# Layer 0's product taken from a transposed x three tiles ahead, with the channel mix applied to the product; phase-major x and output

## The chip, the cores and the metric

One core of a Trainium2 chip runs the program. The metric is the time of one execution in microseconds on the device; medians of several executions are compared. The profile is that of one execution, whose span runs from the first to the last instruction.

## The reference

Two layers are applied to x (128 batches, 32 channels, 512 features). Each mixes channels or features of a batch and then applies a linear layer over the 512 features with a low-rank part that is chosen per row; both add their result to x.

```python
# layer 0: per-batch channel mix, then linear + 4 gated low-rank experts
agg_w = einsum('bk,koi->boi', att, weight)          # 32x32 per batch, att from an MLP on cond_128
c0 = einsum('boi,bih->boh', agg_w, x) + agg_b[:, :, None]
y0 = c0 @ W_base.T + b_base + sum_e alpha_e * ((c0 @ A_e.T) @ B_e.T) * 2
x1 = x + y0                                         # alpha = softmax over 4 experts of c0 @ router_W
# layer 1: grouped convolution of 9 taps along the features, then linear + top 2 of 28 experts
c1 = conv(x1, weight, groups=4) + ctx + bias
y1 = c1 @ base_W.T + sum_{top 2} gate_e * ((c1 @ A_e.T) @ B_e.T) * 2
out = x1 + y1
```

## The kernel before

A tile is 4 batches, so its 128 rows are 4 x 32 channels; there are 32 tiles (NT). Every engine runs its own program and waits on semaphores. Each has a function `step(s)`, and `steps` calls it for s = -1 or 0 to 33: the first and last ones unrolled, the middle in a loop of four steps. In step s TensorE works on layer 0 of tile s, the convolution of tile s-1, and layer 1 of tiles s-2 (LAG) and s-3. So the order of the calls in `step` is the order of TensorE's work; nothing else plans it.

Layer 0 of tile t goes so. `mix` holds for each tile a block-diagonal 128x128 matrix with the four batches' agg_w. Four plain fp32 matmuls (L866) with a quarter of x as the stationary operand give c0 transposed in `p_c0`. ScalarE rounds it to f32r (`c0_hi`, L478), VectorE takes the rest (`c0_lo`, L620). The linear layer is then done in three f32r passes, hi x hi, hi x lo (`hi_passes`, L713 and L714) and lo x hi (`lo_passes`, L719), over 4 chunks of 128 features: first half with 36 columns for experts and router (292 columns, into `p_y0a`), then `other_half` (256 columns). The router chain on VectorE and ScalarE (L601 to L616, L473) makes g0s; TensorE transposes it (L897), ScalarE copies it to g0t (L487), and two matmuls (L916, L917) add the low-rank part and the biases. VectorE adds x (L638, two halves) to give x1.

x1 goes to a scratch in memory (L365) and comes back as convolution windows (L355, three DMAs). The convolution is 16 plain fp32 matmuls with 32-column stationary operands (L790). VectorE transposes its result (L595), ScalarE rounds it (L470), GpSimd takes the rest (L432). `lows_1` multiplies by 224 low-rank and 28 gate columns (252 columns), VectorE does the top-2 gate chain (L671 to L696), `base_1` is the linear layer (512 columns, 12 matmuls), `transpose_g1` (L804) and `low_rank_1` (6 matmuls of 512 columns) finish the tile, and VectorE adds x1 into `y_sb` (L585), which is stored (L362). x and the output are stored feature by feature, while the kernel works by phase (feature mod 4): L585 and L638 read or write with a stride of 4.

Before step 0 comes a setup: a small MLP on TensorE and ScalarE gives att; eight f32r matmuls (L757) on a stack of hi and lo parts of the weights give all mix matrices, which VectorE (L563) and ScalarE (L461) copy into `mix` in 16 blocks each; eight matmuls (L725, L726) pick the active experts; row sums and biases are folded into b0_stack and z_add (L646, L652); w0, a1 and w1 are split into hi and lo parts on ScalarE, GpSimd and VectorE (L454, L412, L490, L492, L655, L428); b1_hi and b1_lo are made from three matmuls (L923, L927, L928).

## Time and profile before

| what | us |
|---|---|
| median of 3 runs (402.69 to 403.41) | 403.36 |
| span of the profiled execution | 401.6 |
| TensorE busy (share) | 384.2 (96%) |
| VectorE busy | 269.5 (67%) |
| ScalarE busy | 97.4 (24%) |
| GpSimd busy | 77.4 (19%) |
| share of the chain that ended last: TensorE | 90% |
| DMA: 54.65 MB, share of the 16 engines' time | 57.1% |

The profiled execution's own time on the device is not listed apart from its span; the span lies 1.8 us under the median, since it counts from the first instruction to the last and the time of a run also has what lies around them. In the rows further down, a line of the timeline is a start, a duration, the engine, the line of the kernel, the operation, its output and inputs, and a count; in brackets stands the idle time before it and what ended it. A plain fp32 matmul leaves two records, an f32r one a single record. Matmuls overlap, so their pace is read from one start to the next and not from a duration.

### The profile page before, as it was taken

How to read it: one execution, taken by the hardware profiler on the slowest of the kernel's cores; microseconds unless marked ns; L12 is line 12 of the kernel's file. 1: busy time of each engine (PE TensorE's matmuls, PEld its weight loads, DVE VectorE, ACT ScalarE, POOL GpSimd, SP SyncE). 2: the span in 40 equal slices, each digit the busy share in tenths (PEclk: the TensorE clock that was granted, in tenths of full speed). 3: DMA queues.
4: the chain of work that ended last, by engine and by line, in shares of the span. 5: the costliest groups of instructions: out<-in, count | busy, mean ns of one | idle time of the engine just before them, and what ended most of it. 6: DMA issues, size and time to landing. Idle time of an engine off the chain costs nothing.

```text
span 401.6 us, 9219 instructions
## 1 busy us (share of the span) xinstructions
PE 384.2 (96%) x3233; PEld 334.9 (83%) x3233; DVE 269.5 (67%) x891; ACT 97.4 (24%) x287; POOL 77.4 (19%) x124
## 2 busy tenths in 40 slices
PE   4799899999999999999999999999999999999986
PEld 3667788888889988888889988888889888888774
DVE  6696376767766666667766666667766666667655
ACT  5742222211122222211122222211122222212120
POOL 5764111110111111110111111110111111110120
PEclk9999999999999999999999999999999999999999
DMA  7604766565566566655566666655566666654441
GB/s 257 220 2 95 169 132 154 136 146 133 124 153 139 123 157 157 145 127 133 123 153 137 124 157 157 144 125 135 125 153 135 126 157 157 145 125 114 101 95 52
DMA packets 65699, 54.65 MB, mean 136 GB/s; under 512 B 3357, under 2 KB 52733, under 8 KB 65430
## 3 DMA queue, kind: packets, MB, share of 16 engines
q1 hardware_dynamic: 65686, 54.48, 57.1%
q8 instruction: 7, 0.11, 0.1%
q14 instruction: 6, 0.05, 0.1%
HBM read 37.56 MB, written 16.91 MB: 136 GB/s over the span
## 4 chain that ended last, share of the span: by engine, by line
PE 90%; DVE 4%; DMA 2%; issue 2%; ACT 1%; SPq 0%; POOL 0%; DVEq 0%
PE p_y L713 10%; PE p_y L714 10%; PE p_y L719 10%; PE p_y0ab L713 9%; PE p_y0ab L719 8%; PE p_y0ab L714 8%; PE p_cv L790 8%; PE p_c L866 7%; PE p_h L719 4%; PE p_h L713 4%; PE p_h L714 4%; PE p_g L804 2%; DMA win<-x_scratch 1%; PE p_y0ab L916 1%; PE p_c L897 1%
## 5 line engine op out<-in xcount | busy, mean ns | idle before, releaser
L432 POOL TENSOR_TENSOR c_lo<-c,c_hi 128x512 fp32r<-128x512 f32 x32 | 40.7, 1273 | 253.3 <-ACT c_hi L470 253.3
L713 PE MATMUL p_y0ab<-w_hi,c_hi 128*128 128x292 f32 (+1 forms) x256 | 73.9, 316 | 0.5 <-DVE x L638 0.5
L714 PE MATMUL p_y0ab<-w_lo,c_hi 128*128 128x292 f32 (+1 forms) x256 | 67.6, 290 | 0.0
L713 PEld LDWEIGHTS p_y0ab<-w_hi,c_hi 128*128 128x128 f32 x256 | 48.7, 190 | 9.5 <-issue 8.0
L585 DVE TENSOR_TENSOR y_sb<-p_y,x 128x512 f32<-128x512 f32 x31 | 33.5, 1080 | 32.7 <-PE p_y L719 32.7
L713 PE MATMUL p_y<-w_hi,c_hi 128*128 128x512 f32 x124 | 49.4, 398 | 0.0
L714 PEld LDWEIGHTS p_y0ab<-w_lo,c_hi 128*128 128x128 f32 x256 | 49.1, 192 | 0.0
L714 PE MATMUL p_y<-w_lo,c_hi 128*128 128x512 f32 x124 | 49.0, 395 | 0.0
L719 PE MATMUL p_y0ab<-w_hi,c_lo 128*128 128x292 f32 (+1 forms) x256 | 43.1, 290 | 0.0
L470 ACT CAST c_hi<-c 128x512 fp32r<-128x512 f32 x32 | 19.8, 620 | 89.9 <-DVE c L595 89.9
L498 ACT ACTIVATE t_exp<-top,ntop 128x2 f32<-128x2 f32 x32 | 9.5, 296 | 129.6 <-DVE ntop L678 129.6
L638 DVE TENSOR_TENSOR x<-p_y0ab,x_sb 128x256 f32<-128x256 f32 x64 | 35.6, 598 | 3.5 <-PE p_y0ab L917 3.5
L790 PEld LDWEIGHTS p_cv<-win,wc_sb 96*32 96x32 f32 x1024 | 26.0, 109 | 13.7 <-issue 10.7
L719 PEld LDWEIGHTS p_y0ab<-w_hi,c_lo 128*128 128x128 f32 x256 | 36.7, 190 | 0.0
L790 PE MATMUL p_cv<-win,wc_sb 96*32 96x128 f32 x1024 | 34.6, 276 | 1.8 <-DMA win<-x_scratch 1.8
L866 PE MATMUL p_c<-mix,x_sb 128*128 (+1 forms) x256 | 35.4, 283 | 0.0
L719 PE MATMUL p_y<-w_hi,c_lo 128*128 128x512 f32 x124 | 34.0, 396 | 0.0
L866 PEld LDWEIGHTS p_c<-mix,x_sb 128*128 128x128 f32 x256 | 33.3, 199 | 0.0
L713 PE MATMUL p_h<-a_hi,c_hi 128*128 128x252 f32 x128 | 31.7, 281 | 0.0
L714 PE MATMUL p_h<-a_lo,c_hi 128*128 128x252 f32 x128 | 31.5, 280 | 0.0
L595 DVE STREAM_TRANSPOSE c<-p_cv 128x512 f32<-128x512 f32 x32 | 22.9, 716 | 12.1 <-PE p_cv L790 12.1
L601 DVE TENSOR_TENSOR z<-p_y0ab,z_add 128x36 f32<-128x36 f32 x32 | 6.2, 194 | 34.9 <-PE p_y0ab L719 34.9
(182 smaller groups left out, 683.2 us busy)
## 6 DMA issues: line engine op xcount, KB each, us to landing
win<-x_scratch SPq DMA_DIRECT2D x96, 256.0 KB, 4.4
x_scratch<-x SPq DMA_DIRECT2D x32, 260.0 KB, 2.1
x_sb<-in_x SPq DMA_DIRECT2D x32, 256.0 KB, 5.1
out<-y_sb SPq DMA_DIRECT2D x32, 256.0 KB, 2.1
w_sb<-in_w SPq DMA_DIRECT2D x2, 1024.0 KB, 8.6
exp_sb<-in_experts SPq DMA_DIRECT2D x1, 512.0 KB, 4.7
a_sb<-in_a SPq DMA_DIRECT2D x1, 504.0 KB, 8.1
b_sb<-in_b SPq DMA_DIRECT2D x1, 448.0 KB, 11.7
```

What stands on the lines that cost most here:

```text
L432: pool.tensor_tensor(by_group(c1_lo[:, v.mod(2)]), by_phases(c1), by_group(c1_hi[:, v.mod(2)].bitcast(f32)), ALU.subtract).then_inc(c1_lo_ ...
L470: nc.scalar.copy(by_group(c1_hi[:, v.mod(2)]), by_phases(c1)).then_inc(c1_hi_done, 1)
L498: nc.scalar.activation(t_exp[:], top[:, 0:2], ACT.Exp, bias=ntop[:], accum_out=t_sum[:]).then_inc(t_exp_done, 1)
L585: V.tensor_tensor(y_sb[:, v.mod(2), :].rearrange("p (q f) -> p f q", f=NPH), y1_bank(v).rearrange("p (f q) -> p f q", f=NPH), x1[:, v.mod( ...
L595: V.transpose(c1[:], p_cv[:]).then_inc(c1_tr, 1)
L638: last = V.tensor_tensor(x1[:, s.mod(4), phases, 1:1 + NQ], p_y0[n].rearrange("p (f q) -> p f q", q=NQ), x_sb[:, s.mod(4), :].rearrange("p ...
L713: mm(psum, lhs_hi, rhs_hi, start=start and n == 0, stop=False)
L714: mm(psum, lhs_hi, rhs_lo, start=False, stop=False)
L719: last = mm(psum, lhs_lo, rhs_hi, start=False, stop=stop and n == len(operands) - 1)
L790: last = mm(p_cv[rows, :].rearrange("p (b g m) -> p b g m", b=BT, g=GROUPS)[:, :, g], wc_sb[:, g, :], win[:, v.mod(2)].rearrange("p (b g) ...
L804: last = nc.tensor.transpose(p_g1t[:, a, :], g1[:, a, :], ident[:])
L866: last = mm(p_c0[:, cols], x_sb[:, t.mod(4), cols], mix[:, t.n(), :], start=True, stop=True)
```

## The change

Layer 0's linear layer and channel mix are exchanged: mixing acts on the rows and the linear layer on the features, so (mix x) W = mix (x W). The host passes x also transposed (`xt`), 128 features by 128 rows for each of 4 chunks. TensorE computes u = x W in three f32r passes with the quarters of xt as stationary operands (`u_half`, halves "b" and "a") three tiles ahead (UA), ScalarE rounds xt (`xt_high`) and copies u out of PSUM (`u_copy`), GpSimd takes xt's low part (`xt_low`) and copies the tile's mix matrix (`mix_copy`). In step s two plain fp32 matmuls of 292 and 256 columns (`mixing`) apply the mix matrix to u. Step 0 computes u of tiles 1, 2 and 3, and u of tile 0 is computed in the setup; steps 29 to 31 compute none.

In the setup, seven matmuls of `ones` by `ones`, whose result nobody reads, come first on TensorE. w0 is loaded in four quarters that ScalarE and VectorE split; the f32r stack of the attention weights is gone, and eight plain fp32 matmuls take its place. The mix blocks are copied in two parts, those of tiles 0 to 3 in the setup and the others in step 0; z_add likewise. w1 is loaded into w0's buffer once that is free, and split in step 1; b1 comes with a row of zeros from the host, which a row sum of w1 fills in step 2, instead of three matmuls. x and the output are phase-major in memory (the host rearranges them), so that both additions on VectorE are one contiguous operation of 512 columns; the addition of x now comes after the gate chain on VectorE. `at(s, c)` is true in the unrolled step c. Layer 1's computation is the same, but its gate product comes before u and its transpose at the step's end.

```diff
+            sp.dma_start(xt_sb[:, 0, :], xt[0]).then_inc(xt_loaded[0], 16)
+            for c in range(HC):
+                sp.dma_start(w_sb[:, c, :], w0[:, c * D:(c + 1) * D]).then_inc(ld_w0[c], 16)
...
+            sp.dma_start(xt_sb[:, 1, :], xt[1]).then_inc(xt_loaded[1], 16)
+            sp.dma_start(bb_sb[:], b_base).then_inc(ld_bb, 16)
+            sp.dma_start(xt_sb[:, 2, :], xt[2]).then_inc(xt_loaded[2], 16)
             sp.dma_start(x_sb[:, 0, :], x_v[0]).then_inc(x_loaded[0], 16)
+            sp.dma_start(xt_sb[:, 3, :], xt[3]).then_inc(xt_loaded[3], 16)
...
+            sp.wait_ge(xt_lo_done, 1)
+            sp.dma_start(xt_sb[:, 0, :], xt[4]).then_inc(xt_loaded[0], 16)
+            sp.wait_ge(w0_lo_done, HC)
+            sp.wait_ge(w0_pairs_done, 1)
+            sp.dma_start(w_sb[:], w1.rearrange("p (c d) -> p c d", c=HC)).then_inc(ld_w1, 16)
+            sp.wait_ge(a0_mm, 1)
+            sp.wait_ge(b0_mm, 1)
+            sp.dma_start(b1_sb, b1.rearrange("p (a d) -> p a d", a=2)).then_inc(ld_b1, 16)
...
+                if (s + 5).live():
+                    t = s + 5
+                    after(sp, xt_lo_done, t, -4)
+                    sp.dma_start(xt_sb[:, t.mod(4), :], xt[t.n()]).then_inc(xt_loaded[t.mod(4)], 16)
...
+            def xt_low(t):
+                after(pool, xt_hi_done, t)
+                pool.tensor_tensor(xt_lo[:, t.mod(2)], xt_sb[:, t.mod(4)], xt_hi[:, t.mod(2)].bitcast(f32),
+                                   ALU.subtract).then_inc(xt_lo_done, 1)
...
+                after(pool, mixed_mm, t, -4)
+                pool.tensor_copy(mix_t[:, t.mod(4)], mix[:, t.n(), :]).then_inc(mixt_done, 1)
...
+                if at(s, 0):
+                    xt_low(s + 3)
+                if (s + 2).live():
+                    mix_copy(s + 2)
+                if (s + 4).live():
+                    xt_low(s + 4)
...
+            def xt_high(t):
+                after_dma(act, xt_loaded, t)
+                after(act, u_mm, t, -2, 2, 2)
+                nc.scalar.copy(xt_hi[:, t.mod(2)], xt_sb[:, t.mod(4)]).then_inc(xt_hi_done, 1)
+            def u_copy(t, half):
+                part, (banks, cols) = "ba".index(half) + 1, HALVES[half]
+                after(act, u_mm, t, 0, 2, part)
+                after(act, mixed_mm, t, -4)
+                nc.scalar.copy(u[:, t.mod(4), cols], p_u[:, banks]).then_inc(u_done, 1)
...
+                t = s + (1 if at(s, 0) else UA)
+                if t.live():
+                    u_copy(t, "b")
+                if s.live():
+                    after(act, g0_tr, s)
+                    nc.scalar.copy(g0t[:], p_g0t).then_inc(g0t_done, 1)
+                if t.live():
+                    u_copy(t, "a")
+                if at(s, 0):
+                    act.wait_ge(mix_zeroed, 5)
+                    for n, t in enumerate((s + 2, s + 3)):
+                        u_copy(t, "b")
+                        u_copy(t, "a")
+                        if n == 0:
+                            xt_high(s + 4)
+                        mix_copies(REST, [n])
...
                     after_dma(dve, y_stored, v, -2)
-                    V.tensor_tensor(y_sb[:, v.mod(2), :].rearrange("p (q f) -> p f q", f=NPH),
+                    V.tensor_tensor(y_sb[:, v.mod(2), :].rearrange("p (f q) -> p f q", f=NPH),
                                     y1_bank(v).rearrange("p (f q) -> p f q", f=NPH), x1[:, v.mod(4), :, 1:1 + NQ],
                                     ALU.add).then_inc(y_done, 1)
+                def residual(v):
+                    after(dve, y0_mm, v)
+                    after_dma(dve, x_loaded, v)
+                    after_dma(dve, x1_stored, v, -4)
+                    V.tensor_tensor(x1[:, v.mod(4), :, 1:1 + NQ], p_x1.rearrange("p (f q) -> p f q", q=NQ),
+                                    x_sb[:, v.mod(4), :].rearrange("p (f q) -> p f q", f=NPH), ALU.add).then_inc(x1_done, 1)
...
+                if s.live():
+                    residual(s)
+                if at(s, 0):
+                    dve.wait_ge(mix_zeroed, 5)
+                    mix_copies(REST, range(BT // 2, BT))
...
+                    dve.wait_ge(rs1_mm, 1)
+                    V.tensor_copy(rs1[:], p_rs1).then_inc(rs1_done, 1)
+                    dve.wait_ge(a1_hi_done, 1)
+                    V.tensor_tensor(a1_lo[:], a1_sb[:], a1_hi[:].bitcast(f32), ALU.subtract).then_inc(a1_lo_done, 1)
+                    dve.wait_ge(w1_hi_done, 1)
+                    V.tensor_tensor(w1_lo[:], w_sb[:], w1_hi[:].bitcast(f32), ALU.subtract).then_inc(w1_lo_done, 1)
...
+            def u_operands(t, cols):
+                slot = t.mod(2)
+                return [(xt_hi[:, slot, c * P:(c + 1) * P], xt_lo[:, slot, c * P:(c + 1) * P], w0_hi[:, c, cols], w0_lo[:, c, cols])
+                        for c in range(HC)]
+            def u_half(t, half):
+                part, (banks, cols) = "ba".index(half) + 1, HALVES[half]
+                after(pe, xt_hi_done, t)
+                after(pe, u_done, t, -1, 2, part)
+                hi_passes(p_u[:, banks], u_operands(t, cols), True)
+                after(pe, xt_lo_done, t)
+                lo_passes(p_u[:, banks], u_operands(t, cols), True).then_inc(u_mm, 1)
...
+            pe.wait_ge(ones_done, 1)
+            for _ in range(7):
+                mm(p_u[:, 0:P], ones[:], ones[:], start=True, stop=True)
...
+            after(pe, xt_hi_done, first)
+            for c in range(HC - 1):
+                pe.wait_ge(w0_lo_done, c + 1)
+                hi_passes(p_u[:, banks], u_operands(first, cols)[c:c + 1], c == 0)
+            pe.wait_ge(ident_done, 1)
+            pe.wait_ge(att_done, 1)
+            nc.tensor.transpose(p_att, att[:], ident[:]).then_inc(att_t_mm, 1)
+            pe.wait_ge(w0_lo_done, HC)
+            hi_passes(p_u[:, banks], u_operands(first, cols)[HC - 1:HC], False)
+            after(pe, xt_lo_done, first)
+            lo_passes(p_u[:, banks], u_operands(first, cols), True).then_inc(u_mm, 1)
...
             pe.wait_ge(att_t_done, 1)
             for m in range(CH // BT):
-                last = mm(p_y0ab[:, m * BATCH:(m + 1) * BATCH], kw_stack[:, m * BT * CH:(m + 1) * BT * CH], att_t[:],
+                last = mm(p_cvh[:, m * BATCH:(m + 1) * BATCH], kw_sb[:, m * BT * CH:(m + 1) * BT * CH], att_t[:],
                           start=True, stop=True)
...
+            pe.wait_ge(a0_lo_done, 1)
+            u_half(first, "a")
             pe.wait_ge(vmat_done, 1)
-            mm(p_vrow, vmat[:], sel_r[:], start=True, stop=True).then_inc(vrow_mm, 1)
+            mm(p_vrow, vmat[:], sel_r[:], start=True, stop=True)
+            pe.wait_ge(a0_sum_done, 1)
+            mm(p_rs0, ones[:], a0_sum[:], start=True, stop=True).then_inc(zrow_mm, 1)
+            pe.wait_ge(beta1_done, 1)
+            mm(p_b0, sel[:], exp_sb[:, 1, :], start=True, stop=False)
+            pe.wait_ge(w0_sum_done, 1)
+            pe.wait_ge(picks_done, 2)
+            mm(p_b0, pick_rs0[:], w0_sum[:], start=False, stop=False)
...
+                def mixing(v):
+                    if at(v, 0):
+                        pe.wait_ge(rs0_done, 1)
+                        pe.wait_ge(vrow_done, 1)
+                    after(pe, u_done, v, 0, 2, 2)
+                    after(pe, mixt_done, v)
+                    after(pe, x1_done, v, -1)
+                    for half in "ab":
+                        banks, cols = HALVES[half]
+                        mm(p_y0[:, banks], mix_t[:, v.mod(4)], u[:, v.mod(4), cols], start=True,
+                           stop=half == "a").then_inc(z0_mm if half == "a" else mixed_mm, 1)
...
                 if s.live():
-                    after(pe, c0_lo_done, s)
...
-                if s.live():
-                    after(pe, x1_done, s, -1)
-                    first = [(*c0_pairs[c], w0_hi[:, c, 0:Z0N + NY], w0_lo[:, c, 0:Z0N + NY]) for c in range(HC)]
-                    hi_passes(p_y0a[:, 0:Z0N + NY], first, True)
-                    lo_passes(p_y0a[:, 0:Z0N + NY], first, True).then_inc(z0_mm, 1)
-                if (s + 1).live():
-                    t = s + 1
-                    after_dma(pe, x_loaded, t)
-                    if t.i is None and t.c in (0, 1):
-                        pe.wait_ge(mix_act_done, (t.c + 1) * BT * BT // 2)
-                        pe.wait_ge(mix_dve_done, (t.c + 1) * BT * BT // 2)
-                    after(pe, c0_lo_done, s)
-                    for c in range(HC):
-                        cols = slice(c * P, (c + 1) * P)
-                        last = mm(p_c0[:, cols], x_sb[:, t.mod(4), cols], mix[:, t.n(), :], start=True, stop=True)
-                    last.then_inc(c0_mm, 1)
...
+                    mixing(s)
+                if at(s, 0):
                     pe.wait_ge(ld_bb, 16)
-                    mm(p_y1[0:K0, :], pick_rs0[:], w0_sum[:], start=False, stop=False)
-                    mm(p_y1[0:K0, :], pick_bias[:], bb_sb[:], start=False, stop=True).then_inc(b0_mm, 1)
...
-                if (s + -LAG).live() and is_last(s + -LAG):
+                    mm(p_b0, pick_bias[:], bb_sb[:], start=False, stop=True).then_inc(b0_mm, 1)
...
-                if (s + -LAG).live() and not is_last(s + -LAG) and not lows_early:
-                    lows_1(s + -LAG)
-                conv_early = s.i is None and s.c >= NT - 1
-                if (s + -1).live() and conv_early:
-                    conv(s + -1)
-                if (s + -LAG).live() and not is_last(s + -LAG):
-                    base_1(s + -LAG)
-                if (s + -1).live() and not conv_early:
-                    conv(s + -1)
-            steps(pe, step, -1, NT + 2, 3, 7)
+                    low_rank_1(s + -LAG)
+                else:
+                    if (s + -3).live() and not is_last(s + -3):
+                        low_rank_1(s + -3)
+                    if (s + -LAG).live():
+                        lows_1(s + -LAG)
+                    ahead = (s + 1, s + 2, s + 3) if at(s, 0) else (s + UA,)
+                    running = ahead[0].live()
+                    if running:
+                        for n, t in enumerate(ahead):
+                            u_half(t, "b")
+                            if n == 0:
+                                transpose_g0(s)
+                            u_half(t, "a")
+                            if n == 0:
+                                low_rank_0(s)
+                    elif s.live():
+                        transpose_g0(s)
+                    if at(s, 1):
+                        pe.wait_ge(a1_sum_done, 1)
+                        mm(p_rs1, ones[:], a1_sum[:], start=True, stop=True).then_inc(rs1_mm, 1)
+                    if (s + -LAG).live():
+                        if not running and s.live():
+                            base_1(s + -LAG, lambda: low_rank_0(s))
+                        elif is_last(s + -1):
+                            base_1(s + -LAG, lambda: conv(s + -1))
+                        else:
+                            base_1(s + -LAG)
+                    if (s + -1).live() and not is_last(s + -1):
+                        conv(s + -1)
+                    if (s + -LAG).live():
+                        transpose_g1(s + -LAG)
+                if at(s, 2):
+                    pe.wait_ge(b1_lo_done, 1)
+            steps(pe, step, 0, NT + 1, 3, 6)
...
+    rows = i["x"].reshape(NT, P, HC, P)
     return {
-        "x": c(i["x"]), "pack": pack, "kw": c(kw), "experts": c(experts.reshape(P, -1)),
+        "x": by_phase(i["x"]), "xt": c(rows.transpose(0, 3, 2, 1)).reshape(NT, P, HC * P), "pack": pack, "kw": c(kw),
...
+    phased = r.results[0]["out"].reshape(BATCH, CH, NPH, NQ)
+    return np.ascontiguousarray(phased.swapaxes(-1, -2)).reshape(BATCH, CH, D)
```

Three places show the new order. The first is TensorE in the steady loop, where one step ends and the next begins; before the change, around the channel mix:

```order
L719 MATMUL p_y0ab<-w_hi,c_lo 128x292 x4
L866 ISA
L866 MATMUL p_c<-mix,x_sb 128x128 x4
L804 MATMUL p_g<-ident,g 113x128 x2
L713 MATMUL p_y0ab<-w_hi,c_hi 128x256
```

After the change, from the convolution to the low-rank part of layer 1:

```order
L943 MATMUL p_cvh<-win,wc_sb 32x4x32 x16
L956 MATMUL p_t<-ident,g 113x128 x2
L309 REGISTER_ALU
L913 MATMUL p_y<-u,mix_t 128x292
L913 MATMUL p_y<-u,mix_t 128x256
L808 MATMUL p_y<-b_hi,g1t_hi 128x512
```

The mix has moved from between the two halves of the product to the head of the step, behind the transposes of layer 1's gates, and has become two wider matmuls.

The second place is TensorE in the setup, from the picking of experts on. Before:

```order
L757 MATMUL p_y0ab<-att_t,kw_stack 128x128 x8
L761 MATMUL p_cv<-att_t,kw_stack 32x32 x4
...
L768 MATMUL p_g<-sel_r,vmat 128x4
L866 MATMUL p_c<-mix,x_sb 128x128 x4
L873 MATMUL p_c<-a_sum,ones 128x36
L875 MATMUL p_y<-exp_sb,sel 101x512
L713 MATMUL p_y0ab<-w_hi,c_hi 128x292
```

After:

```order
L881 MATMUL p_cvh<-att_t,kw_sb 128x128 x8
L885 MATMUL p_t<-att_t,kw_sb 32x32 x4
L808 MATMUL p_u<-w_hi,xt_hi 128x292
...
L814 MATMUL p_u<-w_hi,xt_lo 128x292 x4
L892 MATMUL p_y<-sel_r,vmat 128x4
L894 MATMUL p_y<-a_sum,ones 128x36
L896 MATMUL p_y<-exp_sb,sel 101x512
L899 MATMUL p_y<-w_sum,pick_rs 101x512
L913 MATMUL p_y<-u,mix_t 128x292
```

Tile 0's product now stands in the setup, half "b" ahead of the picking of experts and half "a" behind the attention matmuls, and the mixing of tile 0 closes the setup.

The third place is VectorE between the router chains of tiles 0 and 1. Before:

```order
L626 SCALAR_TENSOR_TENSOR b_stack<-b_round,minus_lo_row,p_y 101x512
L638 TENSOR_TENSOR x<-p_y0ab,x_sb 128x2x128 x2
L658 COPY rs<-p_g 128x252
L661 TENSOR_TENSOR b_lo<-p_cv,b_hi 113x512
L601 TENSOR_TENSOR z<-p_y0ab,z_add 128x36
```

After:

```order
L736 SCALAR_TENSOR_TENSOR b_stack<-b_round,minus_lo_row,p_y 101x512
L698 TENSOR_TENSOR x<-p_y,x_sb 128x4x128
L624 COPY mix<-p_cvh 32x28x8 x8
L629 TENSOR_TENSOR z_add<-rs,beta 128x1008
L632 TENSOR_TENSOR z_add<-z_add,vrow 128x28x4
L716 TENSOR_TENSOR z<-p_y,z_add 128x36
```

The mix blocks of tiles 4 to 31 and 28 rows of z_add have moved from the setup to a place between two tiles.

## Rows read from the trace of the kernel before

**Rows 1.** The page, parts 1 and 2: busy time of each engine, TensorE by slice, granted clock.

```profile
PE 384.2 (96%) x3233; PEld 334.9 (83%) x3233; DVE 269.5 (67%) x891; ACT 97.4 (24%) x287; POOL 77.4 (19%) x124
...
PE   4799899999999999999999999999999999999986
...
PEclk9999999999999999999999999999999999999999
```

**Rows 2.** Timeline of TensorE, one tile from 200 us: start, duration, engine, line, operation.

```profile
200.29 0.41 PE L713 MATMUL p_y0ab<-w_hi,c_hi 128*128 128x292 f32 x1
...
202.01 1.06 PE L866 MATMUL p_c<-mix,x_sb 128*128 x8
202.90 0.38 PE L804 MATMUL p_g<-ident,g 128*113 128x128 f32 x2
...
204.57 0.48 PE L713 MATMUL p_y<-b_hi,g1t_hi 113*128 113x512 f32 x1
...
207.69 0.40 PE L713 MATMUL p_y<-w_hi,c_hi 128*128 128x512 f32 x1
...
210.58 1.08 PE L790 MATMUL p_cv<-win,wc_sb 96*32 96x128 f32 x32
211.59 0.41 PE L713 MATMUL p_y0ab<-w_hi,c_hi 128*128 128x292 f32 x1
```

**Rows 3.** Timeline of TensorE in setup and the first tiles.

```profile
11.80 1.93 PE L757 MATMUL p_y0ab<-att_t,kw_stack 24*128 24x128 f32 x8 [0.46 <-DVE att_t L552]
...
13.92 0.64 PE L725 MATMUL p_h<-sel,exp_sb 128*128 128x32 f32 x2
...
16.50 2.08 PE L866 MATMUL p_c<-mix,x_sb 128*128 128x128 f32 x8
...
21.41 2.01 PE L875 MATMUL p_y<-exp_sb,sel 128*101 128x512 f32 x2
23.34 0.61 PE L713 MATMUL p_y0ab<-w_hi,c_hi 128*128 128x292 f32 x1
...
26.43 1.62 PE L866 MATMUL p_c<-mix,x_sb 128*128 128x128 f32 x8
...
38.92 1.02 PE L927 MATMUL p_h<-b_sb,ident 112*113 112x512 f32 x2
39.78 1.02 PE L928 MATMUL p_h<-w_sum,pick_rs 128*113 128x512 f32 x2
```

**Rows 4.** Timeline of VectorE, the same tile from 200 us.

```profile
202.33 0.20 DVE L601 TENSOR_TENSOR z<-p_y0ab,z_add 128x36 f32<-128x36 f32 x1 [1.18 <-PE p_y0ab L719]
...
204.09 0.19 DVE L616 TENSOR_TENSOR g0s<-g,g0s 128x32 f32<-128x32 f32 x1
...
208.19 0.24 DVE L671 SCALAR_TENSOR_TENSOR h<-rs,beta,p_h 128x28 f32<-128x28 f32 x1
...
210.95 0.39 DVE L696 TENSOR_TENSOR g<-h,gate 128x224 f32<-128x224 f32 x1
```

**Rows 5.** Groups of instructions by line and shape: line, operation, count, busy us, mean ns, idle before.

```profile
L620 DVE TENSOR_TENSOR c_lo<-p_c,c_hi 128x512 fp32r<-128x512 f32 x32 | 21.8, 683 | 0.0
...
L655 DVE TENSOR_TENSOR a_lo<-a_sb,a_hi 128x1008 fp32r<-128x1008 f32 x1 | 1.2, 1194 | 0.0
...
L575 DVE TENSOR_TENSOR beta<-beta 128x32 f32<-128x32 f32 x1 | 0.8, 784 | 0.0
...
L461 ACT COPY mix<-p_y0ab 32x224 f32<-32x224 f32 x8 | 4.4, 545 | 0.2
...
L492 ACT CAST w_hi<-w_sb 128x2048 fp32r<-128x2048 f32 x1 | 1.9, 1912 | 0.0
...
L432 POOL TENSOR_TENSOR c_lo<-c,c_hi 128x512 fp32r<-128x512 f32 x32 | 40.7, 1273 | 253.3 <-ACT c_hi L470 253.3
```

**Rows 6.** Timelines of VectorE and TensorE near the end.

```profile
376.41 1.13 DVE L638 TENSOR_TENSOR x<-p_y0ab,x_sb 128x256 f32<-128x256 f32 x2
...
385.79 1.08 PE L790 MATMUL p_cv<-win,wc_sb 96*32 96x128 f32 x32 [0.53 <-DMA win<-x_scratch]
```

496 lines of the change are left out of this document (229 added, 267 removed).

## The prediction

> **What bounds the kernel now.** I read the page first. TensorE is busy for 384.2 of the 401.6 us of the span, VectorE for 269.5 [rows 1], so the next question is what TensorE does in one tile and what it loses at the two ends. In the timeline of TensorE in the middle of the run the same instruction comes back after 11.30 us (200.29 to 211.59) [rows 2], and the slices of TensorE read 9 (90% or more) from the sixth to the third last [rows 1]. Inside the period the starts follow one another without a gap: first half of the layer-0 product with its logit columns 1.72 us (200.29 to 202.01), channel mix 0.89 us (202.01 to 202.90), second half with three transposes 1.67 us, low-rank parts of both layers and the low-rank-and-gate product of layer 1 together 3.12 us (by their columns 1.45, 0.24 and 1.43), its base product 2.89 us (207.69 to 210.58), convolution 1.01 us [rows 2]. TensorE is the bound of the tile, and no wait is left there that a new order could remove. What lies outside 32 periods (32 x 11.30 = 361.6) is 40 us: setup, filling and draining the pipeline.
>
> At the start TensorE runs at its lower level (1.2 GHz). The page's row of granted clock shows full speed from the first slice [rows 1], but the intervals contradict it: eight records of the channel mix take 2.08 us at 16.50 and 1.06 us in the steady part, and the twelve matmuls of the first half 3.09 us (23.34 to 26.43) against 1.72. The mix at 26.43 takes 1.62 us, so the level (2.4 GHz from then on) rose inside it, near 27.3 [rows 2, 3]. The useful stream of tile 0 begins at 23.34.
>
> **The steady tile after the change.** Removed: the channel mix on x, 0.89 us. Added: two plain fp32 matmuls of 292 and 256 columns on the product. A plain fp32 matmul of 512 columns takes 0.86 us (38.92 to 39.78) [rows 3], that is 1.68 ns a column, so 548 columns cost 0.92 us. Everything else TensorE does per tile stays. New period: 11.30 - 0.89 + 0.92 = 11.33 us. For the period I take bounds of 11.21 (the convolution is now followed by transposes, and the late start of the f32r matmul after it, 0.12 us of the 1.72, may go) and 11.45 (that much added instead).
>
> Could the new order wait? I walk one step, S = start of the mixing matmuls. They end at S+0.92, layer 1's low rank at S+2.4, its gate product at S+3.8, half b of the product three tiles ahead at S+5.3, half a at S+6.9, layer 0's low rank at S+7.2, base at S+10.1, convolution at S+11.1. VectorE begins, as now, with the transpose of the convolution and g1t_lo, to about S+1.15; then comes the layer-0 router chain of 1.95 us (202.33 to 204.28) [rows 4] to S+3.1; its transpose is asked for at S+5.3. Output addition: the contiguous layout makes it like c_lo, 0.68 us [rows 5], to S+3.8. Gate chain of 3.15 us (208.19 to 211.34) [rows 4] from S+4.05 to S+7.2; its transpose is asked for at S+11.1. Residual 0.68 us to S+8.0; the next mixing wants it at S+11.3. ScalarE gains two copies of the product and one rounding of x and loses one rounding: some 4.1 us of work a step. GpSimd gains x's low part, like the 1.27 us of c_lo [rows 5], and a copy of a quarter of that size. Both stay far under 11.3 us. All slacks are over 0.6 us, the shortest being g0t on ScalarE (ready S+6.3, wanted S+6.9). So the drop in VectorE's work (0.68 of c_lo and 0.4 twice) buys nothing here. The extra load of 256 KB a tile and the rest of the DMAs wait for semaphores that were posted a step before, on SP's queue as well; I cost them at nothing.
>
> **The setup, up to the first mixing (T0).** In the kernel before, the attention chain reaches its matmuls at 11.80 [rows 3]. In the new one the first projection stands behind seven warm-up matmuls (14 records of 0.25 us, ending near 4.7), and VectorE and ScalarE weave four quarters of w0's rounding into the chain; I put the last quarter's low part at 12.5. From there TensorE has: 6 matmuls to finish half b of tile 0; the 8 expert and router matmuls (0.53 us each at the lower level, by the rows at 13.9) [rows 3]; 8 plain fp32 matmuls of 128 columns, i.e. 16 records (0.25 us each at the lower level, 0.111 at the higher) instead of 8; bias rows; half a; two small ones; two of 512 columns. At the higher level: 12.5 + 0.7 + 2.1 + 1.8 + 0.2 + 1.6 + 0.4 + 1.7 = 21.0. At the lower level all of it would be 12.5 + 1.4 + 4.2 + 4.0 + 0.4 + 2.9 + 0.9 + 3.7 = 30.0. Which one holds depends on whether the warm-up matmuls and what follows them raise the level. I take 21.0: the warm-ups run straight into the first projection, so the engine works without a pause from 1.1 to about 5.4, 4.3 us, and the level rose about 4 us after the first matmul of the dense stream at 23.34 [rows 3]; after that no long pause follows. Against it: there, TensorE had been working since 21.0 without the level rising for over 6 us, and what ran first was plain fp32, as the warm-ups are.
>
> The trace cannot decide this. The Trainium skill, "TensorE: Matmul & The Clock Gate" (Part 1), says the default state is throttled and sustained activity releases the throttle. By that rule T0 is 21.0; the rows of the kernel before show only that the level rose late in its own setup.
>
> **The first three steps.** Step 0 holds mixing 0.92, bias row 0.86, three products of 3.1 and low rank 0.24: 11.4 us. Meanwhile VectorE and ScalarE copy the remaining mix blocks, eight each at 0.55 us [rows 5], and VectorE builds 28 rows of z_add, so tile 1's router chain starts near T0+14.9 and its transpose comes at T0+16.5: TensorE waits 2.6 us. Step 1 ends at T0+20.0. Then lows_1 of tile 0 needs the transposed convolution, and on VectorE that is queued behind a1_lo (1.19) and w1_lo (twice as long), which wait for a1_hi and w1_hi (1.91) on ScalarE [rows 5]: it comes at T0+25.6, a wait of 3.7 us. Step 3 begins at T0+35.0. The b1 matmuls of the kernel before (about 2.6 us) are gone; one row sum of 0.86 takes their place.
>
> **The end.** Steps 3 to 28 take 26 x 11.33 = 294.6. Steps 29 and 30 have no product left: 8.24 each, plus a window wait of 0.9: 17.4. x1 of tile 31 comes 7.95 later. From x1 done (377.54) to the last convolution (385.79) it takes 8.25 us, two DMA trips [rows 6]; that path is unchanged and now has less work beside it. After that convolution 15.8 us remained; eight of the twelve matmuls of a base product (1.87) now lie before it and the output addition is 0.4 shorter, but 0.8 more is waited for c1_lo: 14.3.
>
> Sum: 21.0 + 35.0 + 294.6 + 17.4 + 7.95 + 8.25 + 14.3 = 398.5 us of span, against 401.6: 3.1 us less. The median of the three runs, 403.36, lies 1.8 above the profiled span; with the same 1.8 the forecast is **400.3 us**. So three tiles of product moved into the pipeline's start save time at the start, and about half is given back in waits of the first steps and at the end.
>
> **Rivals.** A difference of 0.2% (0.8 us) is about what a measurement tells from none.
> (1) *The clock stays low during setup* (slower). The 14 warm-up records are plain fp32 and the matmuls after them are small and spread; if the level rises only near 24, in half a, T0 is 12.5 + 1.4 + 4.2 + 4.0 + 0.4 + 2.2 + 0.5 + 1.7 = 26.9, and with some waiting 27.3: 406.6 us. It decides from T0 = 24.1 on. For it: the level was low through 7 us of small matmuls (11.8 to 18.6) in the kernel before.
> (2) *VectorE is slowed by GpSimd in the steady tile* (slower). Row L575 took 0.78 us for 32 elements while GpSimd was adding, where L616 took 0.19 for the same size [rows 4, 5]. GpSimd works 3 us per tile in place of 1.7, over the router chain. If its five short operations took 0.6 more each, the chain would end at S+6.1, and TensorE would wait 0.8 us: 26 times, 421.3 us. Against it: the chain has 2.2 us of slack first, and operations that read PSUM were not stretched. By the Trainium skill, "GPSIMD Engine Reference" (1. Specifications), GpSimd shares its SBUF interfaces with VectorE and contends with operations with two SBUF inputs; that agrees with L575.
> (3) *The tile gets cheaper* (faster): 11.21 us each, 26 x 0.12 = 3.1 less: 397.2 us.
>
> **Chances and range.** Forecast 50%, own range 397 to 403 (2.5 for the walk through setup, 1 for the period); rival 1 34%, 404 to 409; rival 2 6%; rival 3 10%. Of the forecast's half 0.43 is faster, 0.04 same, 0.03 slower; rival 3 adds 0.10 to faster; rival 1 0.02 to same and 0.32 to slower; rival 2 0.06. That is 0.53, 0.06, 0.41. The range from 395.5 to 407.5 leaves out rival 2, the upper end of rival 1 and little below.
>
> **What would show it.** Right: warm-ups' successors at 0.11 us per record by 15 us; mixing of tile 0 near 21; starts of the mixing matmuls 11.33 apart; a wait for VectorE's z chain of tile 1 and a longer one before lows_1 of tile 0; the last convolution waiting for its window. Wrong: mixing of tile 0 after 24.1, a period off 11.33 by over 0.1, or waits for x1 in the loop.

## The result

| kernel | median us (lowest to highest, runs) | span of the profiled execution |
|---|---|---|
| before | 403.13 (402.69 to 403.41, 4) | 401.6 |
| changed | 428.80 (428.69 to 429.74, 4) | 427.1 |

The changed kernel takes 1.0646 times as long (95% interval 1.0631 to 1.0661): 25.7 us slower, where 400.3 was forecast. The sum of the prediction, 398.5 us of span, is 28.6 us short. It was made in four pieces, and each can be read from the starts of the mixing matmuls (L913), which stand at 32.25 for tile 0, 80.24 for tile 3, 378.77 for tile 29 and 396.17 for tile 31:

| piece | forecast | measured | difference |
|---|---|---|---|
| setup, to the first mixing (T0) | 21.0 | 32.25 | +11.25 |
| steps 0 to 2 | 35.0 | 47.99 | +13.0 |
| steps 3 to 28 (26 periods) | 26 x 11.33 = 294.6 | 26 x 11.48 = 298.5 | +3.9 |
| steps 29 and 30, and the end | 17.4 + 30.5 | 17.4 + 30.9 | +0.4 |

```profile
32.25 1.29 PE L913 MATMUL p_y<-u,mix_t 128*128 128x292 f32 x4
...
80.24 1.09 PE L913 MATMUL p_y<-u,mix_t 128*128 128x292 f32 x4
...
378.77 1.09 PE L913 MATMUL p_y<-u,mix_t 128*128 128x292 f32 x4
...
396.17 1.09 PE L913 MATMUL p_y<-u,mix_t 128*128 128x292 f32 x4
```

The profile's page of the changed kernel, against [rows 1], shows more busy time on TensorE and a clock that dips in two places:

```profile
PE 397.5 (93%) x3123; PEld 336.0 (79%) x3123; DVE 275.1 (64%) x829; ACT 117.2 (27%) x352; POOL 118.0 (28%) x187
...
PE   5698619999999999999999999999999999999976
...
PEclk9559967999999999999999999999999999999999
```

Cut at the places where the granted clock changes or a step begins, the stretches that matter read so (stretch, length, busy us and instructions of TensorE, its weight loads, VectorE, ScalarE and GpSimd, mean granted clock, share of the DMA engines, GB/s):

```profile
5.30:8.70 3.40, 1.27 (x6) 0.89 (x6) 1.77 (x6) 1.88 (x5) 1.26 (x1) 1.00 0.95 303
8.70:15.00 6.30, 2.05 (x6) 1.08 (x5) 5.67 (x8) 2.41 (x5) 5.76 (x4) 0.50 0.99 370
15.00:32.20 17.20, 17.13 (x66) 14.07 (x67) 7.01 (x21) 3.12 (x12) 4.76 (x8) 0.50 0.20 64
...
45.50:56.50 11.00, 4.55 (x31) 3.93 (x29) 3.80 (x9) 3.85 (x10) 2.71 (x4) 1.00 0.06 25
56.50:70.10 13.60, 7.40 (x42) 3.57 (x42) 9.05 (x11) 5.40 (x10) 10.21 (x8) 0.50 0.76 162
```

Three things stand in it. From 15.0 to 32.2 TensorE works without a pause, at 1.2 GHz: the level had risen at 5.3 us and was gone at 8.7. From 45.5 to 56.5 every engine idles most of the time while the DMA engines are at a share of 0.06, that is one sixteenth. And from 56.5 to 70.1 the clock is low again. The waits of TensorE name what it idled for (us in total, times, longest):

```profile
PE p_cvh L943 <- DMA win<-x_scratch: 7.4, 4, 5.3
PE p_y L929 <- ACT g0t L559: 6.3, 2, 5.1
PE p_u L808 <- DVE w_lo L617: 5.5, 4, 2.3
```

**Step 1 (45.56 to 66.20).** The wait of 5.1 us for g0t is put down to ScalarE, but ScalarE was waiting too, for a load. Its timeline:

```profile
56.20 0.62 ACT L489 CAST xt_hi<-xt_sb 128x512 fp32r<-128x512 f32 x1 [7.01 <-DMA xt_sb<-in_xt]
56.84 0.37 ACT L496 COPY u<-p_u 128x256 f32<-128x256 f32 x1
57.11 0.27 ACT L559 CAST g0t<-p_t 101x128 fp32r<-101x128 f32 x1
```

The queue of SP, which issues the loads and stores, shows what stood ahead of that load:

```profile
34.64 0.25 SPq L364 DMA_DIRECT2D exp_sb<-in_b  x1
34.94 5.67 SPq L376 DMA_DIRECT2D x_sb<-in_x  x1
40.66 1.20 SPq L380 DMA_DIRECT2D xt_sb<-in_xt  x1
41.90 1.26 SPq L387 DMA_DIRECT2D x_scratch<-x  x1
56.90 1.51 SPq L373 DMA_DIRECT2D win<-x_scratch  x3
```

b1 is issued at 34.64, into 113 partitions (112 rows and the new row of zeros). What follows it on the same queue needs 5.67 us to be issued, the transposed x of tile 5 (xt, issued by 41.9) arrives near 56.2, 14 us after its issue, and the store of x1 of tile 0, issued by 43.2, is only done at 56.9, when the windows can be read. For most of the time in between, from 46.5 to 54.5, the DMA engines move 26 GB/s:

```profile
46.50:54.50 8.00, 3.55 (x26) 3.10 (x24) 2.80 (x9) 2.57 (x6) 1.79 (x3) 1.00 0.06 26
```

At that rate (25 GB/s) the 452 KB of b1 take 18 us, from about 36 to 54. My theory (A) was that this one load is carried by one engine. The rival (B): the queue was backed up by bytes.

**The steady tile.** Four mixings in a row are 11.45, 11.45, 11.45 and 11.60 us apart. In one tile of the changed kernel the pieces from one start to the next are: g1's transposes 0.31, mixing 0.74, layer 1's low-rank part (`low_rank_1`) 1.57, its 252 low-rank and gate columns (`lows_1`) 1.39, half b with g0's transpose 1.46, half a 1.73, layer 0's low rank 0.34, base 2.89, convolution 1.01. Taken over the region from g1's transposes to the end of half b, without g0's transpose (0.03), that is 5.44 us, against 4.52 for the same pieces before: the mixing costs 0.92 as forecast. Most of the surplus is at layer 0's low rank, 0.34 in place of 0.24. TensorE there, ScalarE and VectorE, from three timelines:

```profile
211.82 0.27 PE L922 MATMUL p_t<-ident,g0s 128*101 128x128 f32 x1
...
213.58 0.38 PE L929 MATMUL p_y<-b_stack,g0t 101*128 101x256 f32 x1
213.80 0.28 PE L930 MATMUL p_y<-b_stack,g0t 101*128 101x256 f32 x1
```

```profile
212.72 0.30 ACT L552 ACTIVATE t_exp<-top,ntop 128x2 f32<-128x2 f32 x1 [3.77 <-DVE ntop L756]
...
213.01 0.35 ACT L496 COPY u<-p_u 128x256 f32<-128x256 f32 x1
213.26 0.27 ACT L559 CAST g0t<-p_t 101x128 fp32r<-101x128 f32 x1
```

```profile
209.70 1.23 DVE L728 CAST g0s<-g 128x64 fp32r<-128x64 f32 x1
```

g0 is transposed at 211.82, but its copy waits on ScalarE behind the exponential of layer 1's top two (`t_exp`), which waits for VectorE. g0t is ready at 213.53, and the weight load that needs it cannot run ahead. VectorE is late because its cast of the gates takes 1.23 us (0.20 before, as a group 1.035 against 0.195) while GpSimd makes c's and x's low parts.

### The profile page after: what moved, and what is told of

The parts are those of the page before. It is cut to its first block, busy times and chain, and to the rows that moved or that the text cites. A ratio compares the mean times of both kernels' runs of the same rounds, so it can differ in the third digit from the quotient of the medians.

```text
span 427.1 us, 9296 instructions
## 1 busy us (share of the span) xinstructions
PE 397.5 (93%) x3123; PEld 336.0 (79%) x3123; DVE 275.1 (64%) x829; ACT 117.2 (27%) x352; POOL 118.0 (28%) x187
## 4 chain that ended last, share of the span: by engine, by line
PE 79%; DMA 8%; DVE 5%; issue 3%; SPq 2%; ACT 1%; POOL 0%; POOLq 0%; DVEq 0%; ACTq 0%
PE p_y L808 9%; PE p_y L814 9%; PE p_y L809 9%; PE p_cvh L943 7%; PE p_u L814 7%; PE p_u L808 7%; PE p_u L809 7%; PE p_y L913 6%; DMA x_scratch<-x 4%; PE p_cvh L814 3%; PE p_cvh L808 3%; DMA win<-x_scratch 3%; PE p_cvh L809 3%; PE p_t L956 3%; PE p_y L929 2%
## 5 line engine op out<-in xcount | busy, mean ns | idle before, releaser
L808 PE MATMUL p_u<-w_hi,xt_hi 128*128 128x256 f32 (+1 forms) x256 | 71.9, 306 | 5.5 <-DVE w_lo L617 5.5
L809 PE MATMUL p_u<-w_lo,xt_hi 128*128 128x256 f32 (+1 forms) x256 | 68.4, 293 | 0.0
L808 PEld LDWEIGHTS p_u<-w_hi,xt_hi 128*128 128x128 f32 x256 | 49.1, 192 | 7.3 <-DVE w_lo L617 4.7
L809 PEld LDWEIGHTS p_u<-w_lo,xt_hi 128*128 128x128 f32 x256 | 49.2, 192 | 0.0
L420 POOL TENSOR_TENSOR xt_lo<-xt_sb,xt_hi 128x512 fp32r<-128x512 f32 x32 | 41.2, 1288 | 24.5 <-ACT xt_hi L489 24.5
L814 PE MATMUL p_u<-w_hi,xt_lo 128*128 128x256 f32 (+1 forms) x256 | 43.8, 294 | 0.0
L943 PE MATMUL p_cvh<-win,wc_sb 96*32 96x128 f32 x1024 | 35.4, 280 | 7.4 <-DMA win<-x_scratch 7.4
L814 PEld LDWEIGHTS p_u<-w_hi,xt_lo 128*128 128x128 f32 x256 | 37.4, 193 | 0.0
L913 PE MATMUL p_y<-u,mix_t 128*128 128x256 f32 (+1 forms) x128 | 36.2, 406 | 0.0
L728 DVE CAST g0s<-g 128x64 fp32r<-128x64 f32 x32 | 33.1, 1035 | 1.1
L808 PE MATMUL p_cvh<-a_hi,c_hi 128*128 128x252 f32 x128 | 31.4, 280 | 1.0 <-ACT c_hi L539 1.0
L698 DVE TENSOR_TENSOR x<-p_y,x_sb 128x512 f32<-128x512 f32 x32 | 21.9, 685 | 12.2 <-PE p_y L930 12.0
```

Source lines behind the costliest of these rows:

```text
L420: pool.tensor_tensor(xt_lo[:, t.mod(2)], xt_sb[:, t.mod(4)], xt_hi[:, t.mod(2)].bitcast(f32), ALU.subtract).then_inc(xt_lo_done, 1)
L698: V.tensor_tensor(x1[:, v.mod(4), :, 1:1 + NQ], p_x1.rearrange("p (f q) -> p f q", q=NQ), x_sb[:, v.mod(4), :].rearrange("p (f q) -> p f q ...
L728: V.tensor_copy(g0s[:, 0:3 * L0N].rearrange("p (a n) -> p a n", n=L0N)[:, 0:3:2, :].bitcast(f32r), g0[:].unsqueeze(1).to_broadcast([P, 2, ...
L808: mm(psum, lhs_hi, rhs_hi, start=start and n == 0, stop=False)
L809: mm(psum, lhs_hi, rhs_lo, start=False, stop=False)
L814: last = mm(psum, lhs_lo, rhs_hi, start=False, stop=stop and n == len(operands) - 1)
```

## The experiments

The four causes were taken apart first, each with one edit of the changed kernel (428.80 us, T0 32.25, mixing of tile 3 at 80.24, period 11.48).

**e1_b1_rows.** b1 in two loads:

```diff
-sp.dma_start(b1_sb, b1.rearrange("p (a d) -> p a d", a=2)).then_inc(ld_b1, 16)
+sp.dma_start(b1_sb[1:K1], b1[1:K1].rearrange("p (a d) -> p a d", a=2)).then_inc(ld_b1, 16)
+sp.dma_start(b1_sb[0:1], b1[0:1].rearrange("p (a d) -> p a d", a=2)).then_inc(ld_b1, 16)
```

> The load of b1 (113 rows of 4 KB) is split into one of 112 rows and one of a single row; nothing else differs from the changed kernel (428.8 us). Theory A: the load into 113 rows is carried by one of the 16 DMA engines (from about 36 to 54 us the trace shows 25 GB/s at a DMA share of 0.06, one sixteenth), and the loads and the store queued behind it on that engine land only after it. Split, x of tile 5 lands before 46 us, TensorE's waits of 5.07 us (g0t) and 5.27 us (first window) go, about 11 us; the wait before the first low-rank product of layer 1 that was forecast (3.7 us) then appears: 418 to 421 us. Rival B: the queue is backed up by the bytes ahead of it (1 MB of w1 and b1 itself), whatever their rows: 427.5 to 430 us, both waits as before.

Measured: 424.60 us (423.81 to 429.72), ratio to before 1.0577 (1.0509 to 1.0645). SP's queue, and what the 8 us from 46.5 look like now:

```profile
34.88 0.33 SPq L364 DMA_DIRECT2D exp_sb<-in_b  x1
...
35.59 0.35 SPq L377 DMA_DIRECT2D x_sb<-in_x  x1
...
42.72 1.41 SPq L374 DMA_DIRECT2D win<-x_scratch  x3
```

```profile
46.50:54.50 8.00, 2.64 (x18) 2.40 (x17) 6.07 (x9) 3.93 (x10) 6.41 (x6) 0.92 0.36 89
```

The same 452 KB no longer hold anything up: the next issue takes 0.35 us in place of 5.67, and the windows are asked for at 42.72 in place of 56.90. Theory A stands, B falls. Both waits that it named are gone, and the step from the second to the third mixing takes 12.76 in place of 20.64. But the time fell by 4.2 us and not by 8 to 11, for two new waits came: 3.08 us before layer 1's first low-rank product, as forecast, and one that was not, 5.36 us for g0s of tile 1 on VectorE (2.31 in the changed kernel). VectorE and GpSimd in that wait:

```profile
51.34 2.26 DVE L732 TENSOR_TENSOR g0s<-g,g0s 128x32 f32<-128x32 f32 x1
```

```profile
51.22 2.34 POOL L434 TENSOR_TENSOR w_pair<-w_sb 128x1024 f32<-128x1024 f32 x1
```

An operation that takes 0.19 us by itself ends at 53.60, that of GpSimd at 53.56; the cast before it (1.18 us) ends in the same way with GpSimd's low part of x. With the load out of the way GpSimd gets to w1's sum just when VectorE works on the gates. Of the 42.6 us that the three steps still take, step 0 has 13.1, step 1 12.8 and step 2 16.7, where the forecast had 11.4, 8.6 and 15.0: what is left of the miss stands mainly in step 1.

**e2_fill.** Matmuls on `ones` in TensorE's pauses of the setup, 7 behind the attention scores, 10 behind the second quarter of tile 0's half b, 5 behind the transpose of the attention weights:

```diff
+def filler(n):
+    for _ in range(n):
+        mm(p_cvh[:, 0:P], ones[:], ones[:], start=True, stop=True)
...
+filler(7)
...
+filler(10)
...
+filler(5)
```

> 22 more 128x128 plain fp32 matmuls on ones, into columns of a PSUM tile that is not yet used: 7 after the attention scores, 10 after the second quarter of tile 0's product, 5 after the transpose of the attention weights. They fill TensorE's pauses of 1.6, 2.3 and 1.3 us between 6.7 and 15.1 us. Theory A: the granted clock fell to 1.2 GHz at 8.7 us because TensorE paused; with the pauses filled it stays at 2.4 GHz, the 17.2 us from 15.0 to the first mixing take some 8.5, and the first mixing starts near 23.7: 419 to 422 us. Rival B: the narrow matmuls of the setup (4 to 128 columns) bring the level down, or keep it down, whatever came before: first mixing at 30 to 33, 427 to 430 us.

Measured: 423.77 us (422.64 to 425.55), ratio 1.0528 (1.0501 to 1.0556). The first mixing is at 26.48, between the two theories. Two of the stretches of 5 us; the granted clock is the number before the DMA share:

```profile
5.00:10.00 5.00, 4.01 (x22) 3.82 (x23) 2.98 (x10) 3.45 (x8) 1.68 (x2) 0.74 0.95 315
...
20.00:25.00 5.00, 5.00 (x32) 4.43 (x31) 2.00 (x10) 2.57 (x10) 0.29 (x1) 0.66 0.01 5
```

The level still fell before 10 us (the pauses of the attention chain, 0.79 and 0.46 us, had no fillers) and again at 21.1. That second fall came with no pause of TensorE since 15.45, behind a dense half of a product and then matmuls of 4, 32 and 128 columns. So filling the pauses gave 5.8 us of T0 and did not hold the level; that the narrow matmuls brought it down is what their place suggests, no run without them shows it.

**e3_g0t_first.** On ScalarE the exponential behind g0t:

```diff
-if (s + -LAG).live():
-    after(act, ntop_done, s, -LAG)
-    nc.scalar.activation(t_exp[:], ...)
...
 if s.live():
     after(act, g0_tr, s)
     nc.scalar.copy(g0t[:], p_g0t).then_inc(g0t_done, 1)
+if (s + -LAG).live():
+    after(act, ntop_done, s, -LAG)
+    nc.scalar.activation(t_exp[:], ...)
```

> On ScalarE the exponential of layer 1's top two (which waits for VectorE's gate chain) is put behind the copy of the transposed gates of layer 0 (g0t), which TensorE waits for. Theory A: the steady tile takes 11.48 us in place of 11.33 because g0t is copied at 213.26, behind the exponential that came free at 212.72, while its transpose was done near 211.95: period 11.33 to 11.36, about 3.5 to 4 us less in all: 424.5 to 425.5 us. Rival B: the extra 0.15 us is the price of going from plain fp32 to f32r and back: within 0.5 us of 428.8, period 11.45 to 11.48.

Measured: 427.31 us (425.00 to 429.60), ratio 1.0621 (1.0568 to 1.0673). By the times alone this is not told from the changed kernel. The median is in neither expected range, and the runs spread over 4.6 us. The trace does tell: from the fourth mixing to tile 29 every period is 11.32 or 11.33 us, and g0t is copied 0.47 us after its transposition started, not 1.44:

```profile
210.35 0.27 PE L922 MATMUL p_t<-ident,g0s 128*101 128x128 f32 x1
...
212.08 0.29 PE L929 MATMUL p_y<-b_stack,g0t 101*128 101x256 f32 x1
```

```profile
210.82 0.27 ACT L555 CAST g0t<-p_t 101x128 fp32r<-101x128 f32 x1
```

Theory A stands: the price of the exchange in the steady tile is the forecast 0.03 us, the other 0.15 was a queue. The span of this execution, 423.2, is 3.9 us less than 427.1, about what 26 x 0.15 gives.

**e4_sum_late.** GpSimd's sums of w0 moved:

```diff
 xt_low(Tile(None, 0))
-for c in range(HC):
-    pool.wait_ge(ld_w0[c], 16)
-sum_chunks(w_sb, w_pair[:], w0_pairs_done, w0_sum, w0_sum_done)
 xt_low(Tile(None, 1))
+pool.wait_ge(w0_lo_done, HC)
+sum_chunks(w_sb, w_pair[:], w0_pairs_done, w0_sum, w0_sum_done)
```

> GpSimd's sum of the four quarters of w0 (2.41 and 1.60 us, from 9.2 us on) is moved behind the last low part of w0 on VectorE. Theory A: VectorE's low part of the third quarter took 2.72 us in place of 0.69 because GpSimd was adding; moved, it takes 0.69, the last quarter is ready near 12.5 in place of 15.0, and the first mixing comes 2 to 2.7 us earlier: 425.8 to 427 us. Rival B: the sums and the load of w1 behind them come late for their users, or another wait of setup takes its place: within 0.7 us of 428.8.

Measured: 424.01 us (422.64 to 427.20), ratio 1.0508 (1.0479 to 1.0538). VectorE's low part of the third quarter, in the changed kernel and here:

```profile
9.40 2.72 DVE L617 TENSOR_TENSOR w_lo<-w_sb,w_hi 128x512 fp32r<-128x512 f32 x1
```

```profile
9.63 0.69 DVE L616 TENSOR_TENSOR w_lo<-w_sb,w_hi 128x512 fp32r<-128x512 f32 x1
...
11.63 0.67 DVE L616 TENSOR_TENSOR w_lo<-w_sb,w_hi 128x512 fp32r<-128x512 f32 x1
```

The last quarter is done at 12.30 in place of 15.02, and the first mixing starts at 29.53 in place of 32.25: 2.72 us in both places, theory A to the digit. The profiled execution came out at 425.4 us of span, 1.7 less than the changed kernel, and the median 4.8 less, more than the 1.8 to 3 expected; with the runs spread over 4.6 us the size of the gain at the end stays less certain than that at T0.

**e5_xt_late.** The other way to the steady tile:

```diff
 if (s + 4).live():
+    after(pool, g0_lo_done, s)
     xt_low(s + 4)
```

> The changed kernel with one wait more on GpSimd: the low part of x (1.29 us a tile) begins only after VectorE's layer-0 router chain of the same step, ScalarE's order as it was. Theory A: the period of 11.45 to 11.48 us comes from GpSimd: its subtraction beside the chain stretches VectorE's small operations (the cast of the gates takes 1.23 us in place of 0.19), the logits of layer 1, the exponential behind them and with it g0t come late. Without the overlap the cast takes under 0.7 us and the period is 11.33 to 11.36: 424.5 to 426 us. Rival B: g0t is late by the order on ScalarE alone, and the chain's stretch is covered by other waits: period still 11.45 or more, within 0.7 us of 428.8.

Measured: 425.15 us (421.59 to 429.87), ratio 1.0508 (1.0456 to 1.0560). Periods 11.32 to 11.34 throughout. VectorE's cast:

```profile
208.32 0.20 DVE L729 CAST g0s<-g 128x64 fp32r<-128x64 f32 x1
```

So the two explanations of the steady tile are links of one chain: GpSimd's extra operation lengthens the cast by 1.03 us, VectorE's gate chain starts that much later, the exponential and with it g0t too. Breaking it at either link gives 11.33.

**e6_no_warm.** `for _ in range(7)` before the first projection becomes `range(0)`.

> The changed kernel without its seven warm-up matmuls. Theory A: they buy 2.4 GHz from 5.3 to 8.7 us only, in which TensorE does little but wait for w0's quarters, so nothing is lost without them: 427.5 to 429.5 us, first mixing at 32 to 32.5. Rival B: what they set off matters later, and without them the level stays low beyond 32.6 us: 430 to 434 us.

Measured: 428.61 us (427.13 to 434.26), ratio 1.0605 (1.0584 to 1.0626). Theory A: seven warm-ups with nothing dense behind them bought nothing that these runs can tell. In the profiled execution the first mixing came later, at 34.11, by a mishap on VectorE that shows the coupling with GpSimd at its plainest: 8 elements a partition took 4.18 us, until 17.49, beside a subtraction of GpSimd's and its four memsets, the last of which ended at 17.46. The granted clock rose only at 31.9 us here; the level of 5.3 to 8.7 us was the warm-ups'.

```profile
13.31 4.18 DVE L651 TENSOR_SCALAR att<-am_exp,am_rec 128x8 f32<-128x8 f32 x1
```

```profile
14.27 3.19 POOL L443 MEMSET mix<- 128x896 f32 x4
```

**e7_four.** The edits of e1, e3 and e4 together, and fillers of 3, 2, 7 and 4 matmuls, now also in the pauses of the attention chain.

> Four edits together: b1 loaded as 112 rows and one, w0's sums on GpSimd behind VectorE's low parts, g0t ahead of layer 1's exponential on ScalarE, and fillers on TensorE (3, 2, 7 and 4 matmuls of 128 columns in the pauses up to 12 us). If the four causes are independent, their gains add: first mixing at 21 to 24 us, mixing of tile 3 some 42.6 later (as with b1 split alone), 26 periods of 11.33 (294.6), then 17.4 and 30.9: span 406.5 to 409.5, time 408 to 411 us. If they overlap (the level of the clock falls elsewhere, other waits take their place): 412 to 420 us.

Measured: 411.21 us (410.23 to 414.18), ratio 1.0230 (1.0188 to 1.0272); 408.4 us of span. First mixing at 22.84, that of tile 3 another 43.0 us on, 26 periods of 11.33, then 17.1 and 30.9. The gains add up: 17.6 us, against 15.5 for the sum of the four medians by themselves (the fillers are not those of e2, so the 2.1 us more are no sign that one edit helps another). The median is 0.2 us above the range expected.

**e8_more.** The waits of the first steps. GpSimd:

```diff
 if (s + 4).live():
+    after(pool, g0_lo_done, s)
     xt_low(s + 4)
...
 if at(s, 1):
+    after(pool, g0_lo_done, s)
     pool.wait_ge(ld_w1, 16)
```

and on VectorE `z_rows(REST, 2)` from the end of step 0 to that of step 2, w1's low part from step 1 to behind tile 2's router chain; on ScalarE a1's rounding ahead of `u_copy(t, "a")`.

> The four edits of the run before, and the waits of the first steps attacked: GpSimd's sum of w1 and every low part of x only after the router chain of the same step; VectorE builds the remaining 28 rows of additions in step 2 and w1's low part behind tile 2's router chain, so that neither tile 1's chain nor the transpose of tile 0's convolution is queued behind them; ScalarE rounds a1 earlier. Theory A: the waits before g0's transposition in step 1 (5.4 us) and before the first low-rank product of layer 1 (3.1 us) fall under 1 us each, the level stays at 2.4 GHz through these steps, and the mixing of tile 3 comes 31 to 34 us after the first: span 395 to 399, time 397 to 401 us, below the kernel before (403). Rival B: these engines have as much to do in the first three steps wherever it is put; at least one wait of 3 us or more remains or a drop of the clock: 403 to 410 us.

Measured: 405.96 us (403.77 to 410.05, 10 runs), ratio 1.0060 (1.0036 to 1.0084). The wait before layer 1's first product is 0.19 us in place of 2.71 in e7; that for g0s is 2.32 in place of 5.36 and so over my 1 us; 37.0 us from the first to the fourth mixing, where 31 to 34 were expected. The time is that of rival B. What is left of it stands on ScalarE, where tile 1's exponential is queued behind the remaining mix copies:

```profile
42.01 2.25 ACT L504 COPY mix<-p_cvh 32x224 f32<-32x224 f32 x4
44.28 0.30 ACT L544 ACTIVATE z_exp<-z,z_nmax 128x4 f32<-128x4 f32 x1
```

In the profiled execution the level fell at 15.1 us and rose only near 28.7, the first mixing came at 27.14: the same code until then as e7, where the fall came at 17.2 and lasted 3.4 us. The ten runs, spread over 6.3 us, follow their mean granted clock: 0.992 in the three fastest, 0.974 in the two slowest.

**e9_best and e10_nofill.** e9 is e8 with three moves on ScalarE: `xt_high(s + 3)` of step 0 behind g0t, `mix_copies(REST, [1])` from step 0 to behind g0t of step 1, the copy of w1's row sum ahead of layer 1's exponential. e10 is e9 without the 16 fillers.

> The run before, e8, with three more moves on ScalarE: in step 0 the rounding of x of tile 3 behind g0t (TensorE waited 1.20 us for g0t), in step 1 the second half of its remaining mix copies behind g0t (the exponential of tile 1 was queued behind them, TensorE waited 2.32 us), in step 2 the copy of w1's row sum ahead of layer 1's exponential (TensorE waited 1.03 us). Theory A: the three waits go, 4 us less than e8 at the same level of the clock: mixing of tile 3 some 33 us after the first mixing, which comes at 22.5 to 27 us by what the clock does: span 398 to 403, time 400 to 405, median 401.5, at or below the kernel before (403.0). Rival B: the work that is pushed back (the mix copies stand before a1's rounding and the first convolution) costs as much later: 404 to 407 us.

> e9 without the 16 fillers in TensorE's pauses; the seven warm-up matmuls stay. Theory A (the clock of the setup is worth 5 to 7 us and is lost in the pauses): the level falls near 8.7 us and the first mixing comes at 28.5 to 30: 405 to 409 us, 3 to 7 more than e9. Rival B: with the shorter pauses the warm-ups alone hold the level, or the fillers hold nothing: within 1.5 us of e9.

Measured: e9 403.01 us (399.60 to 404.72, 12 runs), ratio 0.9995 (0.9973 to 1.0017); e10 406.80 us (406.60 to 407.36), ratio 1.0091 (1.0077 to 1.0106). Steps 0 to 2 take 31.4 us in e9 and 32.3 in e10. The median of e9 lies in the range of theory A, 1.5 us above its middle: no difference from the kernel before. 1.0 us is given back in step 3 (12.36), where the additions that VectorE makes at the end of step 2 delay the transpose of a convolution (in e8 the convolution itself came later and step 3 took 11.33). Without the fillers the first mixing is at 29.53, with them at 24.63; of these 4.9 us the medians keep 3.8. The fastest run of e9, 399.60 us, has a mean granted clock of 0.996, the slowest, 404.72, one of 0.983.

**e11_before_warm.** The kernel before, with fillers of 7, 3, 2 and 20 matmuls at its start.

> The kernel before (403.0 us) with 32 matmuls on ones at its start: 7 as warm-ups, 3 and 2 in the pauses of the attention chain, 20 behind it. It tells whether a raised clock in the setup is to be had without the rest of the change. Theory A: the level is 2.4 GHz through the setup; the mix's eight records take 1.06 in place of 2.08 us, half the product of tile 0 1.72 in place of 3.09, its mix 0.89 in place of 1.62, which is 2 to 4 us: 399 to 401 us. Rival B: the level falls back in the pauses between 12 and 23 us: 402.3 to 403.7 us.

Measured: 407.34 us (407.20 to 407.64), ratio 1.0108 (1.0094 to 1.0123): slower, which neither theory said. Two rows tell why:

```profile
7.66 4.71 PE L732 MATMUL p_cv<-ones 128*128 128x128 f32 x40
...
20.83 2.05 PE L875 MATMUL p_c<-mix,x_sb 128*128 128x128 f32 x8 [1.47 <-DVE mix L563]
```

I took the pause before 11.8 us for empty. It held the first four expert matmuls (7.66 to 9.8 in the kernel before), and the 20 fillers pushed them behind 12.2. And the level was lost all the same: the eight records of the mix take 2.05 us, as in [rows 3], and come 4.3 us later. So this run doesn't tell what a raised clock would be worth to the kernel before.

**e12_last.** e9, with `z_rows(REST, 2)` in VectorE's pause of step 1, and half b of tile 1's product in the setup, right behind half a of tile 0:

```diff
 u_half(first, "a")
+u_half(first + 1, "b")
...
+if at(s, 0):
+    u_half(s + 1, "a")
+    transpose_g0(s)
+    u_half(s + 2, "b")
+    low_rank_0(s)
+    u_half(s + 2, "a")
+    u_half(s + 3, "b")
+    u_half(s + 3, "a")
```

> e9 with two moves more: VectorE builds the remaining 28 rows of additions in step 1, in the 2.3 us in which it idled (in e9 they stood at the end of step 2, made the transpose of tile 1's convolution late and cost 1.0 us in step 3), and half b of tile 1's product goes ahead of the first mixing, so that three dense halves follow one another in the setup. Theory A: step 3 takes 11.33 again, and the longer dense stretch raises the clock's level no later than in e9: 1 to 3 us less, median 400 to 402 us, faster than the kernel before (403.1) by 0.3 to 0.8%. Rival B: the level falls in the narrow matmuls as it did and rises later, or the additions in step 1 delay x1 of tile 1 and with it the second mixing: 402.5 to 404.5 us, no difference from e9.

Measured: 401.37 us (400.30 to 401.93, 6 runs), ratio to before 0.9952 (0.9938 to 0.9966). It beats both kernels, the one before by 0.5%. That margin rests on the clock of the setup: e9 without its fillers (e10) is 0.9% slower than the kernel before, and what the same clock would give that kernel no run tells (e11). First mixing at 24.25, 30.05 us to that of tile 3, step 3 at 11.33. Its runs lie within 1.6 us, those of e9 within 5.1. At its end some 3 us are lost again: the window of one of the last convolutions is waited for, and the level falls once more, at 375.4, while TensorE idles there (33.8 us from the last mixing to the end, 30.9 in the changed kernel). Why this window comes late here stays open.

```profile
375.49 1.93 PE L961 MATMUL p_cvh<-win,wc_sb 96*32 96x128 f32 x32 [2.17 <-DMA win<-x_scratch]
```

## Why the prediction was wrong

**The steady tile was right as work, wrong as a queue (+3.9 us).** The term 11.30 - 0.89 + 0.92 holds: mixing costs 0.92 by the pieces, and e3 and e5 run at 11.33. The walk failed at two steps. It put VectorE's router chain at 1.95 us, as before; it took 3.5 (207.63 to 211.16), which is the mechanism of rival 2 at half its size: 1.6 us more, where the rival supposed 3. And it gave g0t on ScalarE 0.6 us of slack ("ready S+6.3, wanted S+6.9"): with S = 206.69 it was ready at S+6.84, since the walk left out that g0t is queued behind the exponential of layer 1. VectorE's logits of layer 1, and so the exponential, stand behind the router chain on VectorE. The chain's slack was counted up to its own user (g0's transposition, S+5.3); the second user behind it was overlooked. The upper bound of 11.45 was passed by 0.03. (The 421.3 us of rival 2 should read 421.1 by its own terms, 26 x 0.8.)

**The setup (+11.25 us) is rival 1, and more.** The reason given for 21.0, that after the warm-ups "no long pause follows", was wrong: TensorE paused for 1.62, 0.30, 2.29 and 1.28 us for w0's quarters and 0.45 us for the attention weights, the level was gone at 8.7 us, and the matmuls that the forecast priced at the higher level ran at the lower:

```profile
12.18 0.58 PE L808 MATMUL p_u<-w_hi,xt_hi 128*128 128x256 f32 x1 [2.29 <-DVE w_lo L617]
...
15.07 0.58 PE L808 MATMUL p_u<-w_hi,xt_hi 128*128 128x256 f32 x1 [1.28 <-DVE w_lo L617]
```

Two terms make it up. "The last quarter's low part at 12.5" came at 15.02, 2.5 us later, because GpSimd summed w0 beside VectorE (e4 takes 2.7 back). The other 8.7 are the level: 17.2 us from there to the mixing, against 8.5 forecast at the higher level and 17.5 at the lower. Fillers win part of them back, and how much changes from one execution to the next: the first mixing is at 29.53 in e4 and in e10, which have none, and at 22.84 (e7), 27.14 (e8) and 24.63 (e9) with the same 16. So the forecast's level was to be had only in part, and only by work that the prediction did not have. The rival, though, let the level rise at half a, near 24, for 27.3; it rose at 32.6. Of the rule of the Trainium skill that the prediction cited ("TensorE: Matmul & The Clock Gate", Part 1) the trace agrees as far as the rise at 5.3 us behind the warm-ups, which e6 without them does not have. It does not bear out the rest: from 15.0 us on TensorE was busy for 17.13 of 17.20 us and the throttle was not released until 32.6, so the 21.0 us that were read from the rule did not come.

**The first three steps (+13.0 us) failed at the sentence on DMAs**, "I cost them at nothing". b1's load got one row more, 113 in place of 112, which the description of the change had in words and the sum left out. That row is worth 5.4 of the 13.0 us by itself: without it (e1) the steps take 42.6 us. e8 and e9 show what it covered: with the queues of VectorE, GpSimd and ScalarE in another order as well they take 37.0 and then 31.4. The forecast waits were of the right kind (2.6 us for z's chain of tile 1: 2.31; 3.7 before layer 1's first product: nothing while the load covered it, 3.08 when it did not), but their sum was too small, since each was walked with operations at their undisturbed durations, and g0t's wait of 1.20 us in step 0 was missed.

The Trainium skill states the rule that was overlooked: "DMA: Bandwidth & Descriptors" ("Why a DMA increments its semaphore by 16 and not by 1") says that a copy is split over the largest number of engines up to 16 that divides the outermost sizes of its two patterns. By it 112 rows go to 16 engines and 113, a prime, to one. The trace agrees: a DMA share of 0.06 at 25 GB/s with 113 rows, and no trace of it in e1. It would have made a rival with a price, as an estimate: 452 KB at a sixteenth of the 370 to 430 GB/s that the setups of both kernels reach (370 over 8.7 to 15.0 us of the changed one, 432 over 9 to 12 us of the one before), 17 to 20 us of a blocked queue.

**The end** was right to 0.4 us.

**The changes of the clock after 56.5 us** came behind the wait: TensorE had been busy for 4.55 of 11 us. They made the convolution, the mixing and the row sum that followed twice as long (1.93, 2.20 and 1.86 against 1.08, 1.09 and 1.02). None of it was priced.

## What to carry to other kernels

A load's number of partitions belongs into the costing of a change as much as its bytes: one row more on 112 left it to one DMA engine of sixteen and held up all that was queued behind it. In an engine's queue every operation that waits is checked against what stands behind it, at durations that hold beside its neighbours' work: g0t stood behind an exponential of another layer, and that behind a chain which GpSimd had stretched. Matmuls that only keep TensorE busy help in pauses that are truly empty (e10 against e9: 3.8 us, with runs spread over 5.1) and cost their whole length in one that only seems so (e11: 4.3 us).

## What was not expected of the hardware

- VectorE's small operations in SBUF can wait for GpSimd's whole instruction and not just slow down by a share: 1.23 us for 64 elements, 2.26 for 32, 4.18 for 8, each ending within 0.1 us of the end of an instruction of GpSimd (209.70 + 1.23 = 210.93 beside 210.87; e1 and e6 above). The 4.18 us ran beside five instructions of GpSimd's, one behind the other. Operations of 512 elements were touched too (2.72 in place of 0.69). Not all were: the two additions of 512 columns that read PSUM kept their 0.69 us, and the reduction and the reciprocal of the router chain kept their 0.16 us in every tile in which they ran beside GpSimd (25 and 30 of 32). The Trainium skill's page "GPSIMD Engine Reference" (1. Specifications) names contention with instructions in a two-port mode or with two SBUF inputs; that the wait lasts to the end of GpSimd's instruction is seen here.
- TensorE was busy for 17.13 of 17.20 us, 15.0 to 32.2, and the level stayed at 1.2 GHz. What ran was narrow (4 to 128 columns, on as few as 8 and 16 rows) in the first half, then a dense half of a product, narrow ones again, and two of 512 columns, behind which it rose. In e7 the level fell at 17.2 us, just behind such matmuls, for 3.4 us.
- The mean granted clock of a run is no measure where a kernel starts low: e10 shows 1.000 in three runs of 406.6 to 407.0 us, e9 one of 0.987 in 402.87 us. Before the first change of level the record reads as full speed, as in [rows 1].
- How the changed kernel's own spread comes about stays open: its fourth run, 429.74, has a mean clock of 0.98 and the other three 0.952 to 0.956, which would fit a run in which the warm-ups never raised the level; no profile of such a run was taken.
